# Second feed-forward weight split among the last gelu blocks, and the last attention pair combined earlier on GpSimd, in a one-core transformer layer

## The reference

```
x = x + attention(layernorm(x))            # w_qkv (256, 3072), w_out (1024, 256)
h = gelu(layernorm(x) @ w1 + b1)           # w1 (256, 1024)
x = x + (h @ w2 + b2) * sum(top2 weights)  # w2 (1024, 256), router_w (256, 8)
```

## Time and profile before

| | us |
|---|---|
| median of 3 runs | 1180.0 (1179.93 to 1180.29) |
| time of the profiled execution | 1180.13 |
| its span | 1178.3 |
| PE busy | 1164.7 (99%) |
| DVE busy | 976.0 (83%) |
| ACT busy | 873.4 (74%) |
| POOL busy | 667.0 (57%) |

### The profile page before, as it was taken

One profiled execution on the slowest core, in us unless ns is written; L12 is line 12 of the kernel. 1 busy time (PEld: TensorE's weight loads), 2 busy tenths in 40 slices (PEclk: granted clock), 3 DMA queues, 4 the chain that ended last, 5 costly groups with the idle time before them and its releaser, 6 DMA issues.

```text
span 1178.3 us, 28904 instructions
## 1 busy us (share of the span) xinstructions
PE 1164.7 (99%) x11195; PEld 1024.6 (87%) x11195; DVE 976.0 (83%) x1736; ACT 873.4 (74%) x1897; POOL 667.0 (57%) x826
## 2 busy tenths in 40 slices
PE   9999999999999999999999999999999998999999
PEld 6778888888888888888888888888888887998898
DVE  7888898888888888888888988898889887777764
ACT  6888888888888888888888888888888885334432
POOL 5776565655566655656565566565656585223321
DMA  4233111411141114111411132113211334334321
GB/s 128 61 88 105 35 33 34 122 35 38 37 127 37 38 37 127 37 38 37 126 38 37 38 111 53 37 38 89 69 33 32 87 90 150 127 110 144 110 74 36
DMA packets 74663, 83.08 MB, mean 71 GB/s; under 512 B 12576, under 2 KB 67360, under 8 KB 74528
## 3 DMA queue, kind: packets, MB, share of 16 engines
q1 hardware_dynamic: 74528, 81.24, 25.7%
HBM read 31.14 MB, written 16.25 MB: 40 GB/s over the span
## 4 chain that ended last, share of the span: by engine, by line
PE 87%; POOL 3%; DVE 3%; ACT 2%; issue 1%; DVEq 0%; POOLq 0%; ACTq 0%
PE ps L551 43%; PE ps L622 18%; PE ps L608 11%; PE ps L574 9%; PE ps L580 4%; DVE pT_lo L1090 1%; POOL prob L964 1%; DVE negmax L1174 1%; ACT prob L878 1%; PE ps L737 1%; POOL attT_lo L1001 1%; POOL att_hi_v L995 0%; POOL wout_lo L985 0%; ACT wbig_hi L906 0%; POOL attT_hi L964 0%
## 5 line engine op out<-in xcount | busy, mean ns | idle before, releaser
L964 POOL TENSOR_SCALAR prob<-prob,rowinv 128x512 f32<-128x512 f32 x512 | 354.9, 709 | 239.3 <-DVE rowinv L1179 238.8
L878 ACT ACTIVATE prob<-ps,negmax 128x512 f32<-128x512 f32 x512 | 346.8, 685 | 36.0 <-DVE negmax L1174 32.4
L1090 DVE TENSOR_TENSOR pT_lo<-ps,pT_hi 128x512 fp32r<-128x512 f32 (+1 forms) x384 | 320.3, 862 | 18.8 <-ACT pT_hi L871 13.9
L1174 DVE TENSOR_REDUCE negmax<-ps 128x2 f32<-128x1024 f32 x256 | 311.0, 1215 | 1.3 <-PE ps L580 1.3
L868 ACT ACTIVATE pT_hi<-ps 128x1024 fp32r<-128x1024 f32 x128 | 131.6, 1028 | 99.8 <-issue 99.1
L608 PEld LDWEIGHTS ps<-identity,prob 64*128 64x128 f32 x4096 | 154.4, 138 | 57.8 <-issue 20.4
L608 PE MATMUL ps<-identity,prob 64*128 64x64 f32 x4096 | 177.3, 226 | 2.4 <-DVE vbuf L1090 1.3
L574 PE MATMUL ps<-nat 64*128 64x512 f32 x1024 | 171.2, 412 | 0.3 <-DVE nat L1091 0.3
L622 PE MATMUL ps<-pT_hi,vbuf 128*128 128x256 f32 x1024 | 164.8, 283 | 2.2 <-DVE pT_lo L1090 2.1
L622 PE MATMUL ps<-pT_lo,vbuf 128*128 128x256 f32 x1024 | 164.5, 283 | 0.0
L622 PEld LDWEIGHTS ps<-pT_hi,vbuf 128*128 128x128 f32 x1024 | 144.9, 191 | 8.6 <-DVE pT_lo L1090 3.3
(11 more groups left out here) (112 smaller groups left out, 2292.5 us busy)
## 6 DMA issues: line engine op xcount, KB each, us to landing
att_hi_v<-halves_out SPq DMA_DIRECT2D x128, 128.0 KB, 2.3
att_lo_v<-halves_out SPq DMA_DIRECT2D x128, 128.0 KB, 2.4
blocks_scratch<-xblocks SPq DMA_DIRECT2D x15, 512.0 KB, 5.0
xn<-blocks_scratch SPq DMA_DIRECT2D x60, 128.0 KB, 2.8
xin<-in_x SPq DMA_DIRECT2D x32, 128.0 KB, 3.2
xres<-in_x SPq DMA_DIRECT2D x8, 512.0 KB, 4.2
x_scratch<-xres SPq DMA_DIRECT2D x8, 512.0 KB, 3.9
xin<-x_scratch SPq DMA_DIRECT2D x32, 128.0 KB, 3.2
```

The lines of the kernel that those rows point to most:

```text
L878: act.activation(prob[:, n % NPROB, j * SEQ:(j + 1) * SEQ], ps[:, PS_SCORE[n % 2] + j, :], ACT.Exp, bias=negmax[:, n % 4, j:j + 1], accum_ ...
L964: return pool.tensor_scalar(dst, src, scalar, 1.0, ALU.mult, ALU.mult)
L1090: return dve.tensor_tensor(dst, full, hi, ALU.subtract)
L1174: dve.tensor_reduce(negmax[:, n % 4, :], ps[:, PS_SCORE[n % 2]:PS_SCORE[n % 2] + 2, :], AX.X, ALU.max, negate=True).then_inc(s_max, 1)
```

## The change

Five things move, and no instruction is added or taken away. The split of w2's first half (chunk 10): ScalarE makes its high part after `transposed_hi(255)` instead of before it, and VectorE its low part after `hidden_lo(2)` instead of before `transposed_lo(255)`. The second half (chunk 11): SyncE loads it after `spread_input(B + 1)` instead of before `store_blocks(B + 1)`, ScalarE makes its high part after gelu block 6 instead of after block 3, and VectorE its low part after `hidden_lo(5)` instead of before `hidden_lo(1)`. GpSimd makes `attention_out(NPAIR - 1)` before `hidden_hi(6)` instead of after `hidden_hi(7)`. VectorE's `ffn_split(1)` stands before `hidden_lo(6)` instead of after `hidden_lo(7)`.

```
-        slot_of_chunks.update({NUNIT - 7: [8], NUNIT - 2: [9], NUNIT + 1: [10], NUNIT + 3: [11]})
+        slot_of_chunks.update({NUNIT - 7: [8], NUNIT - 2: [9]})
...
             spread_input(B + 1)
+            load_weight(sp, 11)
             sp.dma_start(b2_sb[:, :], b2_rows).then_inc(s_b2, 16)
...
+            def split_weight(i):
+                wait_weight_loaded(act, i)
+                act.activation(weight_chunk(i)[1][0], weight_stage(i), ACT.Copy).then_inc(s_whi, 1)
...
                 split_weights(2 * step)
+                if step == LAST_STEP:
+                    split_weight(10)
                 if 0 <= 2 * step < NUNIT and step != 1:
                     exp(2 * step)
...
                     gelu(c * FT + f)
+                    if c == 0 and f == FT - 2:
+                        split_weight(11)
                     if f == (TT - 1 if c else FT - 1) and c + 1 < B:
                         x2_hi(c + 1)
...
                 for f in range(len(HIDDEN_SLOTS) if c == 0 else 0, FT):
+                    if c == 0 and f == FT - 2:
+                        attention_out(NPAIR - 1)
                     hidden_hi(c * FT + f)
-                if c == 0:
-                    attention_out(NPAIR - 1)
...
+            def weight_lo(i):
+                dve.wait_ge(s_whi, i + 1)
+                hi_part, lo_part = weight_chunk(i)[1]
+                lo(lo_part, weight_stage(i), hi_part).then_inc(s_wlo, 1)
...
-                for i in weight_slots(slot):
-                    if i in POOL_CHUNKS:
-                        continue
-                    dve.wait_ge(s_whi, i + 1)
-                    hi_part, lo_part = weight_chunk(i)[1]
-                    lo(lo_part, weight_stage(i), hi_part).then_inc(s_wlo, 1)
...
                     hidden_lo(c * FT + f)
+                    if f == first and c == 0:
+                        weight_lo(10)
                     if f == TT - 1 and c == 0:
                         turn_logits(0)
-                    if f == (TT - 1 if c else FT - 1) and c + 1 < B:
+                    if f == FT - 3 and c == 0:
+                        weight_lo(11)
+                    if f == (TT - 1 if c else FT - 3) and c + 1 < B:
                         ffn_split(c + 1)
```

More of the change, by code:

```diff
@@ L902, in split_weights @@
                 for i in weight_slots(slot):
-                    if i in POOL_HI:
-                        continue
-                    wait_weight_loaded(act, i)
-                    act.activation(weight_chunk(i)[1][0], weight_stage(i), ACT.Copy).then_inc(s_whi, 1)
+                    if i not in POOL_HI:
+                        split_weight(i)
+            def split_weight(i):
+                wait_weight_loaded(act, i)
+                act.activation(weight_chunk(i)[1][0], weight_stage(i), ACT.Copy).then_inc(s_whi, 1)
             for step in range(FIRST_STEP, LAST_STEP + 1):
```

## The result

The changed kernel takes 1182.12 us (median of 22 runs, 1180.84 to 1183.58) against 1180.41 for the kernel before (22 runs, 1179.82 to 1181.12): ratio 1.0014, 95% interval 1.0008 to 1.0019. It is slower by about 1.7 us, where 1.3 us faster was forecast, and outside the range. The profiled execution took 1183.19 with a span of 1181.4.

What follows compares the result with a forecast made beforehand. TensorE, busy 99%, was taken to bound the kernel. Three stalls gone win 4.1 us, two new ones give back 2.8, so 1.3 us from the profiled 1180.13 gives 1178.8, stated as 1178.7; range 1177.2 to 1180.0.

Steps and rivals of the forecast that it cites:

- Slower, by TensorE's clock: Rival: two new stalls around `route(1)` make TensorE's clock fall, costing 2.5 us, total 1181.2 us; chance 0.05.
- the new ones are each no longer than the longest: Argument against the clock rival: neither new TensorE stall exceeds the longest before, 1.66 us, after which it did not slow.
- the two count together: Condition of the clock rival: stalls before `route(1)` and `down(0, 0)` count as one gap, near 3 us idle of 3.9.
- Its price: Clock rival's cost, 2.5 us, taken from 12 matmuls at kernel start: 5.35 us, where 12 at 0.235 are 2.8.
- need as long to come back: Clock rival's assumption: after falling in the new gap, the clock recovers as slowly as at the kernel's start, costing 2.5 us.
- The late load: w2's second half issued at 989.25, lands after 4.4 at 993.65; a 6.2 us chain starts `down(0, 0)` at 999.85.
- the bounds I gave: Uncertainty 0.4 on chain and issue times; landing after 3.9 to 5.1 us; likeliest gains 0.2 to 2.2 us.
- The size of the stalls: New TensorE stalls: about 1.5 us before `route(1)` and 1.4 before `down(0, 0)`, giving back 2.8 us.
- the three old stalls: Stalls before the product with v, `up(0, 6)` and last pair's output all go: 0.99 + 1.33 + 1.82 = 4.14 us.
- the landing's bound of 5.1: Slowest 512 KB transfer: w2's second half would land at 994.35, leaving a gain of 0.6 us.
- the 1.82 that I gave it: Third stall, before the last pair's output: goes as GpSimd makes `attention_out` ahead of two hidden blocks, 1.82 us by starts.
- Nothing later takes part: After `down(0, 0)`: VectorE's and SyncE's later work starts as early as before or earlier, so the gain reaches the end.

Runs made afterwards that it cites:

- first and second filled: Two kernels: changed kernel plus idle-time matmuls on TensorE, ten ahead of `route(1)` only, or four ahead of `down(0, 0)` only; ratios 1.0004 and 1.0006 to the kernel before.
- the same again: The changed kernel measured once more, unaltered, as a reference on the next chip; ratio 1.0019 to the kernel before.
- the first half alone: Kernel before with only the split of w2's first half moved, the second half as before; ratio 1.0039.
- GpSimd's part undone: Changed kernel with `attention_out(63)` again behind GpSimd's high parts of blocks 6 and 7; ratio 1.0049 to the kernel before.
- GpSimd's part alone: Kernel before with only GpSimd's last pair's output made ahead of its high parts of blocks 6 and 7; ratio 0.9989.
- with both: Changed kernel with 14 idle-time matmuls, ten ahead of `route(1)` and four ahead of `down(0, 0)`; ratio 1.0018 to the kernel before.
- with the additions first: Kernels with w2's second half in its own buffer, or loaded ahead of the spreading, plus additions to xres ahead of `hidden_lo(6)` and `hidden_lo(7)`; ratios 0.9981 and 0.9995.
- the load ahead of the spreading: Changed kernel with the load of w2's second half issued ahead of the transfers spreading the next input; ratio 0.9987 to the kernel before.
- the load ahead, the additions ahead, `x2_hi(2)` late: Changed kernel with load ahead of spreading, additions ahead of hidden blocks 6 and 7, `x2_hi(2)` and `ffn_split(2)` behind block 5 of c = 1; ratio 0.9994.

## Why the prediction was wrong

**The rival that came true.** It was the one named "Slower, by TensorE's clock", priced at 2.5 us and given 0.05. The step that failed is its weighing: "the new ones are each no longer than the longest". I worked out 1.5 and 1.4 us; they were 2.52 and 1.15 (the second is 1.3 by starts, in my own sum too), and the condition I named myself, that the two count together, holds (first and second filled). I argued from a kernel in which a stall of 1.66 us had left the clock alone, which says nothing of 3.7 us of standing with 0.9 of work between. The Trainium skill ("TensorE: Matmul & The Clock Gate", section "HAM oscillation") says that waits for transfers between short bursts of matmuls let the clock fall back. The trace of the changed kernel agrees: after a wait that goes back to a transfer, `route(1)` and a second wait the granted clock was 0.50.

**Its price** of 2.5 us fits, and 1181.2 with the 0.84 us below is the 1182 that was measured. But that is in part luck. I took it from 12 matmuls at the kernel's start, where only their spacing, some 0.43 us, speaks for the lower level: the granted clock of that stretch, 1.44 to 6.79 us, reads 1.00 in the trace. And "need as long to come back" is no fixed number of matmuls. In each of the four profiles that show a fall (the changed kernel, the same again, the first half alone, GpSimd's part undone) the clock was low for 6.8 us, and what that costs depends on how much of it is work: some 5.7 us in the changed kernel, 3.1 with GpSimd's part undone.

**The late load.** The mechanism was right, term for term: load, high part, gelu 7, `x2_hi(1)`, `ffn_split(1)`, blocks 6 and 7, three additions. From landing to `down(0, 0)` the chain took 1001.80 - 995.62 = 6.2 us, as summed. Two terms were too small. The load was issued 0.3 us late, because VectorE's normalising took 1.68 instead of 1.37; GpSimd's hidden blocks ran beside it, but no run tests whether they are the reason. And it landed after 4.95, not 4.4. Both are inside the bounds I gave (0.4 and 5.1; the changed kernel again took 5.2), and together they made `down(0, 0)` 0.84 us later than forecast, 22.50 after the last turned tile instead of 21.66. So 0.5 us of the 1.3 were left before the clock took 2.5. By the fit that the Trainium skill gives ("DMA: Bandwidth & Descriptors", section "Anatomy of one DMA") the load would have landed after 3.2 us, an estimate by that page; the loads of w2's second half took 3.9 to 5.2 in all profiles here.

**The size of the stalls.** `route(1)` started 20.26 us after the last turned tile, where the sum had 19.4: all of the 0.84 lay ahead of it. TensorE itself was there after 17.6 instead of 17.9: my sum of the three old stalls was 0.3 too small, since the first matmuls after a stall also run 0.1 us longer than the next ones (989.73 to 990.07 is 0.34, where the others are 0.23 apart). So by starts the first stall was 2.68 and not 1.5, and the second as forecast (2.24 us from `route(1)` to `down(0, 0)`, forecast 2.25). I should have put the landing's bound of 5.1 through the stalls too, not only through the end: it gives a first stall of 2.2 us, longer than any the clock had survived.

**The three stalls** were right: all went, and GpSimd's part alone is worth 0.0011, some 1.3 us, of the 1.82 that I gave it (`down(0, 0)` after 21.64 instead of 23.00); the rest waits behind `ffn_split(1)`. But they are not independent. The first half alone makes the kernel slower by 0.4%.

**"Nothing later takes part"** held for the changed kernel, whose clock was down. With the clock up, the same start of `down(0, 0)` brings a wait for the next input, that of c = 2, of 0.2 us with one stall filled and of 1.7 with both, where the store landed late; with the additions first it was 1.2 and 1.5. VectorE's later work did not start later, as I said; but `down(0, 0)` moved ahead of it, and I had looked only for waits in the trace of before and not for how little room there was behind them.

## What to carry to other kernels

When a change trades several short stalls of TensorE for fewer and longer ones, add up the idle time that stands close together, at the slow end of its range; the clock's fall is a step of its own, here 2.5 us for 3.7 of standing, and worth more than the whole gain. Put a weight's load ahead of a queue's other transfers if an engine will stand at it with others' work behind, and count what those other transfers lose by it. And when one gate is opened, look for the next chain that starts at the same place: here TensorE waited for the next input once `down(0, 0)` started 3 to 4 us earlier than before.

## What was not expected of the hardware

- The clock fell some 0.1 us after the last matmul of `route(1)`, all four of which had run at the full level, in the second stall, and 5.7 us of dense matmuls then ran at 1.2 GHz. In the changed kernel, with two stalls of 2.5 (2.8 in its second profile) and 1.15 us and 0.9 of work between, the mean clock of all 33 executions shows a fall. With stalls of 1.12 and 1.16 (the load ahead of the spreading) the mean was under 1.000 in 4 of 11, with one of 2.28 alone in 6 of 11, with one of 1.16 alone in none of 11, with one of 1.10 alone (the load ahead, the additions ahead, `x2_hi(2)` late) in 2 of 11. For the executions without a profile only the mean clock is known, not where it fell.
- In all four profiles with a fall the clock was low for 6.8 us, whether TensorE stood or worked in them.
- The same 512 KB store of the input of c = 2 landed after 2.6, 3.3, 4.5 or 4.9 us in kernels that issue it at the same place. Where it took 4.5 or more, TensorE had been filled on both sides of `route(1)`; a cause was not tested.
